# Seven half-width block products in place of eight for each pair of sparse chunks, with half of the second product before it placed between the sixth and the last two

## The reference, cut to what matters

```python
x = _layernorm(x + _L0_attn_ref(x, ...))      # Taylor terms and a gated FFN of width 1248
x = _layernorm(x + _L0_ffn_ref(x, ...))       # the sparse FFN, of width 1792

def _L0_ffn_ref(x, c1_w, c2_w, w1, w2t):
    inter = xf @ c1_w.T @ c2_w.T                                   # rank 16, 1792 scores for each token
    blk = inter.reshape(B * T, n_blocks, SPARSITY)                 # 56 blocks of 32
    idx = jnp.argmax(blk, axis=-1) + jnp.arange(0, INTER, SPARSITY)
    h = jax.nn.relu(jnp.einsum('bkm,bm->bk', w1[idx], xf))
    return jnp.einsum('bk,bkm->bm', h, w2t[idx])
```

## Time and profile before

| what | us |
|---|---|
| median of 3 runs (lowest, highest) | 734.05 (733.7, 734.46) |
| the profiled execution's span | 731.9 |
| TensorE busy in it | 722.7 |
| sparse pairs 0 to 27, from the first block to the last hidden chunk (425.76 to 705.13) | 279.37 |
| from the last hidden chunk to the end of the span | 26.8 |

### The profile page before, as it was taken

The page is one execution under the profiler, slowest core; times in us unless marked ns, Lnnn a source line. Parts: engine busy times, 40 slices in busy tenths (PEclk is TensorE's granted clock), DMA queues, the critical chain, the costliest instruction groups (busy, mean ns, idle before and its releaser), DMA issues.

```text
span 731.9 us, 8884 instructions
## 1 busy us (share of the span) xinstructions
PE 722.7 (99%) x3457; PEld 334.0 (46%) x3457; DVE 480.2 (66%) x930; ACT 214.3 (29%) x341; POOL 157.1 (21%) x131
## 2 busy tenths in 40 slices
PE   8999999999999999999999999999999999999996
PEld 3444444444444444444444444444444444445444
DVE  5978897796877779677767779653755361125136
ACT  1575457435612212122122112122212221122130
POOL 0452443111111111111111111222212212222130
PEclk9999999999999999999999999999999999999999
DMA  9537319310000010100001334104020015001001
GB/s 326 248 124 206 58 15 379 67 48 11 1 17 18 20 20 9 25 20 20 5 19 20 79 81 92 23 4 101 16 75 7 1 29 133 1 0 58 1 1 57
DMA packets 40569, 44.57 MB, mean 61 GB/s; under 512 B 25040, under 2 KB 32848, under 8 KB 39632
## 3 DMA queue, kind: packets, MB, share of 16 engines
q1 hardware_dynamic: 37552, 39.29, 17.9%
q0 software_dynamic: 2112, 4.19, 3.4%
q10 hardware_dynamic: 864, 0.53, 0.2%
HBM read 34.33 MB, written 4.42 MB: 53 GB/s over the span
## 4 chain that ended last, share of the span: by engine, by line
PE 86%; issue 1%; POOL 1%; DVE 0%; ACT 0%
PE acc L469 31%; PE pb L449 24%; PE pa L449 24%; PE acc L775 2%; PE acc L546 2%; PE pick_b L612 1%; PE pick_a L612 1%; POOL big L998 1%; PE pick_a L597 0%; PE pick_b L775 0%; PE acc L465 0%; PE pick_b L465 0%; ACT work L836 0%; ACT work L820 0%; ACT pick_b L821 0%
## 5 line engine op out<-in xcount | busy, mean ns | idle before, releaser
L469 PE MATMUL acc<-big,work 128*128 128x512 f16 x1038 | 234.3, 379 | 0.0
L991 POOL TENSOR_TENSOR work<-work 128x512 f16<-128x512 f32 x92 | 110.2, 1201 | 479.9 <-ACT work L909 270.0
L449 PE MATMUL pa<-xs,big 128*128 128x512 f16 x816 | 188.8, 379 | 0.0
L449 PE MATMUL pb<-xs,big 128*128 128x512 f16 x816 | 187.2, 379 | 0.0
L469 PEld LDWEIGHTS acc<-big,work 128*128 128x128 f16 x1038 | 101.5, 98 | 121.0
L449 PEld LDWEIGHTS pa<-xs,big 128*128 128x128 f16 x816 | 78.6, 98 | 91.8
L449 PEld LDWEIGHTS pb<-xs,big 128*128 128x128 f16 x816 | 78.5, 98 | 91.6
L964 ACT ACTIVATE work<-work 128x512 f16<-128x512 f32 x52 | 32.6, 627 | 203.1 <-DVE work L1611 203.1
L546 PE MATMUL acc<-big 128*128 128x512 f16 x336 | 73.9, 379 | 0.3 <-DVE big L1228 0.2
L1611 DVE SCALAR_TENSOR_TENSOR work<-big,const_sb,pa 128x512 f32<-128x512 f16 x28 | 20.8, 744 | 74.0 <-PE pa L449 67.4
L909 ACT ACTIVATE work<-work 128x512 f16<-128x512 f32 x40 | 25.2, 630 | 143.8 <-DVE work L1365 143.8
(11 more groups left out here) (176 smaller groups left out, 548.8 us busy)
## 6 DMA issues: line engine op xcount, KB each, us to landing
big<-in_w_all SPq DMA_DIRECT2D x2, 3840.0 KB, 17.2
big<-spread_rows SPq DMA_DIRECT2D x16, 448.0 KB, 9.1
big<-in_x_t SPq DMA_DIRECT2D x16, 256.0 KB, 8.7
rows<-in_x POOLq DMA_DIRECT2D x4, 1024.0 KB, 11.8
big<-in_w_all SPq DMA_DIRECT2D x2, 1536.0 KB, 11.2
out<-rows SPq DMA_DIRECT2D x3, 1024.0 KB, 4.3
big<-in_w_all SPq DMA_DIRECT2D x1, 2048.0 KB, 14.4
big<-in_w_all SPq DMA_DIRECT2D x2, 1024.0 KB, 11.6
```

What stands on the lines that cost most here:

```text
L449: mm = nc.tensor.matmul(dst[:, :], weights(wp)(kc * P, P), x_part16(g, xp, kc), start=(kc == 0 and wp == xp), stop=(kc == KC - 1 and wp == 1))
L469: mm = nc.tensor.matmul(acc[t][:, :], act_part(pair, j, ap, t * P, P), weights(wp)(0, H), start=(first and ap == wp), stop=(last and ap == 1))
L991: nc.gpsimd.tensor_tensor(act_part(pair, j, 1), act32[j], act_part(pair, j, 0), ALU.subtract).then_inc(act_lo, 1)
```

## The change

The pair's hidden product, 256 units by 512 tokens over a width of 512, is treated as a 2 by 2 block matrix (two chunks, two halves of the width, two halves of 256 tokens) and made from seven block products instead of eight, after Winograd. A block product (`block_product`) is 2 pieces of the width, three matmuls each, 6 matmuls of 128x128 weights by 256 columns. Four sums of weight blocks for each pair and four sums of x blocks for each group are needed; POOL makes them (`raise_quad`, 6 instructions: two of 512 columns and four of 256), ACT rounds them to float16 (`sums_high`, 1024 columns) and POOL makes the low part (`lower_quad`, 1024 columns): 15 such jobs, of which five are hung in behind phase 1 pairs (11, 12, 17, 18, 19) and ten behind sparse pairs (0 to 5, 8, 9, 15, 16). ACT copies the first block product, then the two of `pb`, then the sum of the next from PSUM (`take_products`), and DVE (two instructions) and POOL (two, `add_products`) combine them into the two chunks in SBUF, on which the mask now works: both of its inputs are in SBUF. The mask's data comes in two halves a group. The scale of these weights is one bit lower.

The core of the diff:

```diff
+SUM_JOBS = (("w", 0), ("w", 1), ("x", 0, 0), ("x", 0, 1), ("w", 2), ("w", 3), ("w", 4), ("w", 5), ("w", 6),
+            ("x", 1, 0), ("x", 1, 1), ("x", 2, 0), ("x", 2, 1), ("x", 3, 0), ("x", 3, 1))
+JOB_IN_SWIGLU = {11: 0, 12: 1, 17: 2, 18: 3, 19: 4}
+JOB_IN_SPARSE = {0: 5, 1: 6, 2: 7, 3: 8, 4: 9, 5: 10, 8: 11, 9: 12, 15: 13, 16: 14}
...
+            def block_product(dst, weights, moving, first=False):
+                for k in range(KH):
+                    for wp, xp in ((0, 0), (0, 1), (1, 0)):
+                        mm = nc.tensor.matmul(dst, weights(k, wp), moving(k, xp), ...)
+                return mm
+
+            def seven_products(g, u, between, after_first, middle):
...
+                if n:
+                    pe.wait_ge(c11_ready, n)
+                block_product(pa[:, low_half], w_block(0, 0), x_block(0, 0), True).then_inc(p1_ready, 1)
+                if n:
+                    pe.wait_ge(c12_ready, n)
...
+                block_product(pb[:, low_half], w_sum(SLOT_S1), x_sum(SLOT_T1), True)
+                block_product(pb[:, high_half], w_sum(SLOT_S3), x_sum(SLOT_T3)).then_inc(p57_ready, 1)
+                if between is not None:
+                    between(KC // 2)
+                pe.wait_ge(p1_taken, n + 1)
+                block_product(pa[:, high_half], w_block(0, 1), x_block(1, 0))
+                block_product(pa[:, low_half], w_sum(SLOT_S2), x_sum(SLOT_T2)).then_inc(p26_ready, 1)
+                if between is not None:
+                    between(KC - 1)
+                if after_first is not None:
+                    after_first()
+                middle()
+                pe.wait_ge(p57_taken, n + 1)
+                block_product(pb[:, low_half], w_sum(SLOT_S4), x_block(1, 1))
+                block_product(pb[:, high_half], w_block(1, 1), x_sum(SLOT_T4)).then_inc(p34_ready, 1)
...
+                seven_products(g, u, between, after_first, lambda: products((0,)))
+                after_hidden()
+                products((1,))
...
+            def take_products(n):
+                act.wait_ge(p1_ready, n + 1)
...
+                act.activation(p1_kept, pa[:, 0:HT], ACT.Copy).then_inc(p1_taken, 1)
...
+                act.activation(p57_kept, pb[:, :], ACT.Copy).then_inc(p57_taken, 1)
...
+                act.activation(q_kept, pa[:, 0:HT], ACT.Copy).then_inc(q_taken, 1)
+
+            def hidden(g, u, high=None, late=False, early=None):
+                take_products(g * U2 + u)
+                if early is not None:
+                    x1_high(early + (GROUPS - 1) * TPG)
                 for j in range(2):
...
                 if high is not None:
                     x1_high(high + (GROUPS - 1) * TPG)
+                if g * U2 + u in JOB_IN_SPARSE:
+                    sums_high(JOB_IN_SPARSE[g * U2 + u])
...
+            def add_products(n):
+                pool.wait_ge(p57_taken, n + 1)
...
+                step(nc.gpsimd.tensor_tensor(p57_sum, p57_kept[:, 0:HT], p57_kept[:, HT:2 * HT], ALU.add))
+                settle()
+                pool.wait_ge(q_taken, n + 1)
+                pool.wait_ge(act_lo, N1 + 2 * n)
+                nc.gpsimd.tensor_tensor(act32[1][:, HT:GT], p57_sum, q_kept, ALU.add).then_inc(c22_ready, 1)
...
+            for n in range(GROUPS * U2):
+                g, u = n // U2, n % U2
+                add_products(n)
+                if n in JOB_IN_SPARSE:
+                    raise_quad(JOB_IN_SPARSE[n])
                 for j in range(2):
...
+                        low(GROUPS * U1 + n, j, m)
+                if n in JOB_IN_SPARSE:
+                    lower_quad(JOB_IN_SPARSE[n])
...
             def mask_hidden(g, u):
+                n = g * U2 + u
+                dve.wait_ge(q_taken, n + 1)
+                dve.wait_ge(act_lo, N1 + 2 * n)
+                v.tensor_tensor(act32[0][:, 0:HT], pa[:, HT:GT], p1_kept, ALU.add).then_inc(c11_ready, 1)
+                dve.wait_ge(p34_ready, n + 1)
+                v.tensor_tensor(work32[:, HT:3 * HT]..., pb[:, :]..., q_kept..., ALU.add).then_inc(c12_ready, 1)
...
                 for j in range(2):
+                    if j:
+                        dve.wait_ge(c22_ready, n + 1)
-                    v.scalar_tensor_tensor(out=act32[j], in0=spread(g, u * 2 + j), scalar=own_rank, in1=(pa, pb)[j][:, :],
+                    v.scalar_tensor_tensor(out=act32[j], in0=spread(g, u * 2 + j), scalar=own_rank, in1=act32[j],
                                            op0=ALU.is_equal, op1=ALU.mult).then_inc(masked, 1)
...
-    nc = bacc.Bacc("TRN2", target_bir_lowering=False, num_devices=1)
+    nc = bacc.Bacc("TRN2", target_bir_lowering=False, num_devices=1, dynamic_dma_scratch_size=4096)
```

More of the change, by code:

```diff
@@ L72 @@
 X1_SCALE = 2.0 ** 9
+TOP2 = 12
 HID_SCALE = 2.0 ** -17
@@ L429, in _ @@
             send(LAST * TPG + 2)
+            sp.wait_ge(masked, C2 + SPREAD_HALVES[0][1])
+            load_spread(2, 0)
             send(LAST * TPG + 3, False)
@@ L683, in _, with second2 @@
             group1(GROUPS - 1)
-            def second2(g, u, kind, after_first):
+            def second2(g, u, kind, after_first, js):
                 before = g * U2 + u - 1
-                for j in range(2):
+                for j in js:
                     c = (u - 1) * 2 + j if kind != "last" else C2 - 2 + j
@@ L697, in second2 @@
                         after_first()
-            def hidden(dst, c, g, between):
-                split_product(dst, lambda part: w2_part(c, 0, part), g, between).then_inc(hid_ready, 1)
-            def unit2(g, u, after_first, after_hidden, after_third, kind, start=False, between=None):
-                for j, dst in enumerate((pa, pb)):
-                    n = g * C2 + u * 2 + j
-                    if not start:
-                        pe.wait_ge(masked, n - 1)
-                    elif j:
-                        pe.wait_ge(swiglu_ready, N1)
-                    hidden(dst, u * 2 + j, g, between if j == 0 else None)
-                    (after_first, after_hidden)[j]()
-                if kind == "phase 1":
-                    before = GROUPS * U1 - 1
-                    for j in range(2):
-                        pe.wait_ge(act_lo, before * 2 + j + 1)
-                        second_product(before, j, lambda part: w1_part(1 - j, 2, part), False, j == 1,
-                                       done=down_ready if j else None)
-                        if j == 0:
-                            after_third()
-                    return
-                if kind != "none":
-                    second2(g, u, kind, after_third)
@@ new lines, in unit2, with last_gated, products @@
+            def unit2(g, u, after_first, after_hidden, after_third, kind, start=False, between=None):
+                def last_gated(j):
+                    before = GROUPS * U1 - 1
+                    pe.wait_ge(act_lo, before * 2 + j + 1)
+                    second_product(before, j, lambda part: w1_part(1 - j, 2, part), False, j == 1,
+                                   done=down_ready if j else None)
+                    if j == 0:
+                        after_third()
+                def products(js):
+                    if kind == "phase 1":
+                        for j in js:
+                            last_gated(j)
+                    elif kind != "none":
+                        second2(g, u, kind, after_third, js)
+                seven_products(g, u, between, after_first, lambda: products((0,)))
+                after_hidden()
+                products((1,))
@@ L778, in second_tile @@
                     mm.then_inc(sparse_ready, 1)
+            unit2(3, 4, none, none, none, "none")
+            for t in range(2):
+                second_tile(3, t, acc[t][:, :])
+            unit2(3, 5, none, none, none, "none")
+            second_tile(3, 2, acc[2][:, :])
+            for h, bank in enumerate(last_halves):
+                second_tile(3, TPG - 1, bank, h * HALF, HALF)
+            unit2(3, 6, none, none, none, "none")
+            for t in range(2):
+                for u in (4, 5):
+                    second_tile(u, t, acc[t][:, :])
+            for t in range(2):
+                second_tile(6, t, acc[t][:, :], done=True)
             for u in (4, 5, 6):
-                unit2(3, u, none, none, none, "none")
-            for t in range(TPG - 1):
-                for u in (3, 4, 5, 6):
-                    second_tile(u, t, acc[t][:, :], done=(u == U2 - 1))
+                second_tile(u, 2, acc[2][:, :], done=(u == U2 - 1))
             for h, bank in enumerate(last_halves):
-                for u in (3, 4, 5, 6):
+                for u in (4, 5, 6):
                     second_tile(u, TPG - 1, bank, h * HALF, HALF, u == U2 - 1)
@@ new lines, in _ @@
+            for u in range(1, GROUPS * U1):
+                low(u, 0, u * 2)
+                if u in JOB_IN_SWIGLU:
+                    raise_quad(JOB_IN_SWIGLU[u])
+                    lower_quad(JOB_IN_SWIGLU[u])
+                low(u, 1, u * 2 + 1)
```

(11 more changed lines are left out.)

188 lines of the change are left out of this document (152 added, 36 removed).

## The result

The changed kernel takes 773.16 us (median of 4 runs), the kernel before 733.88 on the same chip: 1.0515 times as long, with a 95% interval from 1.0485 to 1.0546. The median counts one disturbed run of 1792.7 us; the three others took 768.93, 773.01 and 773.32 us, and the ratio rests on those three alone. I had said 749.0 and a range from 732 to 760. The sign was right and the size was not: 39.3 us lost where 14.9 were forecast.

What follows compares the result with a forecast made beforehand. TensorE was taken as the bound, busy 722.7 of 731.9 us. Terms -16.7 + 9.2 + 5.7 + 7.8 + 3.1 + 5.8 = +14.9 took the median from 734.05 to 749.0 us, range 732 to 760.

Steps and rivals of the forecast that it cites:

- A: z's chain of 3.9 us covered by only 2.59, five tiles, plus z's weight loads: +9.2 us.
- B: Scores 2 wait for the bank that pick 0 frees, 3.7 us against 2.59, five tiles: +5.7 us.
- D: DVE's long runs exceed TensorE's interval: +3.1 us. Also the moment DVE sees the last two block products (`pb`).
- five dense jobs: The five jobs in phase 1 cost nothing, up to 2 us if DVE's picks slip under POOL.
- C: ACT's rounding between the relus and the copy of the first block product, paid in seven pairs: +7.8 us.
- E: POOL's jobs lengthen DVE's two-input SBUF instructions in the long runs: +5.8 us, bounds 0 and 14.
- The gain: Seven products take 4.59 us in place of 5.18, 0.59 less a pair over 28 pairs: -16.7 us.
- the last pairs' second products only change places: 0: At the sparse stage's end, the last second products cover each other, so moving them costs 0.
- The account of one pair behind D: Last relu ends near D + 3.8, P2 (second block product) can start at D + 4.35; the loop has no slack.
- Most small ones fall where POOL waits for its next copy: In DVE's long runs, only a tenth of the small instructions' possible 17.9 us was counted.
- Rival 2: Masks with two SBUF inputs wait for POOL, 10.8 us on top, 760 us; POOL bounds pairs 0 to 5; chance 0.17.
- Rival 1: C, D and E vanish, stalls for z and scores 2 remain: -1.8 us, or -7 (727); chance 0.17 for faster.

Runs made afterwards that it cites:

- run 6: The changed kernel without its fifteen jobs (plain blocks for sums) and with both halves of the second product behind the last two block products: 722.53 us, 0.9853.
- run 5: The changed kernel in its own order without any of the fifteen jobs, plain blocks standing where the sums stood: 742.94 us, 1.0132.
- run 1: The changed kernel without the ten sparse jobs on POOL and ACT, using the sums of phase 1: 747.82 us, 1.0197.
- run 2: The changed kernel without POOL's part of the ten sparse jobs, ACT's rounding kept, sums of phase 1: 750.06 us, 1.0227.
- run 3: The changed kernel with POOL's ten sparse jobs replaced by fills of similar length that read nothing, ACT's rounding kept: 757.7 us, 1.0331.
- run 4: The changed kernel, everything computed, with both halves of the second product behind the last two block products: 752.82 us, 1.0261.

## Why the prediction was wrong in size

Taken apart by the runs, with each step beside the term that I gave it:

| step | predicted | measured | from runs |
|---|---|---|---|
| seven products, both halves behind, no jobs | -16.7 | -10.8 | 6 |
| a half between: A, B and D | +18.0 | +20.4 | 5 and 6 |
| five dense jobs | 0, up to 2 | +4.9 | 1 and 5 |
| ACT's rounding (C) | +7.8 | +2.2 | 1 and 2 |
| POOL beside DVE (E) | +5.8 | +23.1 | 2 and the change |
| sum | +14.9 | +39.8 | |

The sum is 39.8 and not 39.3 because the kernel before measured 733.3 beside run 6 and 733.9 beside the change.

**The gain.** The mechanism held: 9.77 us a pair, six matmuls in 0.66. TensorE's busy time fell by 15.2 us in run 6 (722.7 to 707.5), 1.5 less than the 16.7; 1.3 us went to the waits that run 6 still has; and 2.8 were lost in the tail. The step that failed there is "the last pairs' second products only change places: 0". The last matmul group starts 7.3 us before the end in the kernel before (start 724.60, span 731.9) and 10.1 us before it in run 6 (start 710.66, span 720.8), 2.8 us more. The reason is in the starts of the last normalisations. The first three of the kernel before, from DVE's timeline:

```profile
713.77 0.55 DVE L1445 TENSOR_SCALAR rows<-rows,small 128x512 f32<-128x512 f32 x1
718.95 0.55 DVE L1445 TENSOR_SCALAR rows<-rows,small 128x512 f32<-128x512 f32 x1
724.13 0.55 DVE L1445 TENSOR_SCALAR rows<-rows,small 128x512 f32<-128x512 f32 x1
```

And of the changed kernel (run 6 has the same spacing: 706.33, 710.05, 713.76):

```profile
756.72 0.55 DVE L1662 TENSOR_SCALAR rows<-rows,small 128x512 f32<-128x512 f32 x1
760.43 0.55 DVE L1662 TENSOR_SCALAR rows<-rows,small 128x512 f32<-128x512 f32 x1
764.14 0.55 DVE L1662 TENSOR_SCALAR rows<-rows,small 128x512 f32<-128x512 f32 x1
```

They stood 5.18 us apart before, TensorE's pace, and stand 3.71 apart now, DVE's own. The work that had been the cover was moved ahead.

**A, B and D were right in kind and nearly in size.** z was put at 6.7 us of waits and 2.5 of weight loads, and 7.9 of waits were measured; scores 2 at 5.7 and 3.9 measured; DVE's long runs at 3.1 and the wait for ACT's copy behind them 3.5. Not in the sum were 2.1 us of waits for SP's queue ahead of z and the 3.7 us of longer matmuls. The account of one pair behind D held: the last relu of pair 18 ends 3.80 us after D (670.33 for 666.53), and P2 starts at D + 4.36. Two slips of the working changed little: 3.8 + 0.43 + 0.2 is 4.43 and not 4.35, and five times 1.1 is 5.5 and not 5.7.

**C was too large.** I let ACT's 1.05 us land whole in seven pairs. The wait for ACT did grow by 5.7 us in run 2, but other waits gave 2.0 back and shorter matmuls 2.3, of which 1.7 is the clock's and no merit of the term: waits that stand one behind another in a loop don't add up.

**E is the step that decided.** It had the right mechanism, the right two rows and the wrong share. "Most small ones fall where POOL waits for its next copy" was the failing sentence: with 7.3 us of job in a pair POOL is busy for 11.5 of the 15.46 us behind pair 1 and for 14.1 of the 15.88 behind pair 8, and DVE's chain of small instructions steps through POOL's sums one by one. L1619 and L1621, six each from 442 to 660 us, cost 2.7 and 4.0 us over the 162 ns they have alone (6 x 0.453, 6 x 0.665), the multiply 4.1 (20 x 0.207 over run 1), the `TENSOR_SCALAR`, which I had not counted, 2.1. Of all 23.1 us DVE's own instructions account for most: it is busy for 545.9 us in the change and for 527.4 in run 2, 18.5 more. The term had counted two-input instructions alone; one-input ones are lengthened too, and they carry most of the 7.6 us that fills cost in run 3. Rival 2, "the lock decides", was right in its title and wrong in its place: it laid the wait on the masks, which bear 1.4 us.

**Dense jobs.** "Up to 2" was 4.9. TensorE's waits at the start of the sparse stage show it: 1.8 us for the last multiply of the gated FFN on DVE (L1582 in the changed kernel) there and in run 1, and none in run 5. Another 2.0 us are lost ahead of that: pair 0's first block product starts at 427.60 us in run 1 and at 425.63 in run 5.

**The clock.** "The clock should stay where it is" failed. The change and run 6 issue the same 3961 matmuls and are busy for 717.8 and 707.5 us. So 10.3 of the 50.4 us between their spans are longer matmuls and 40.1 are idle time. In the change the granted clock was 0.50 in four stretches (438.51 to 441.93, 472.65 to 479.47, 564.81 to 568.22 and 650.14 to 653.55 us) with 15.3 us of busy TensorE, in run 6 in none before its last matmul. Half of 15.3 is 7.7 us, which is what the clock cost; the other 2.6 I cannot place, and the modelled ends of matmuls in front of waits may be part of it. This cost is inside the measured terms above: behind a wait like the 2.59 us in front of pair 3 the loss goes on in the matmuls that follow.

**Rival 1** ("only TensorE's own order counts", 732.3) is the change without jobs, and that measured 742.9: the 10.6 between them are the gain's missing 5.9, the 2.4 by which the order costs more than A, B and D, and D itself, which rival 1 left out (3.1), less the 0.7 between the two medians of the kernel before.

With both halves behind, the fifteen jobs cost 30.3 us too (752.82 - 722.53). Against run 6, run 4 loses 5.5 us ahead of pair 0's D (436.52 for 431.02) and 16.3 in the intervals behind pairs 1, 8 and 15 (16.67, 18.33 and 18.63 us for 11.86, 12.59 and 12.89). DVE is busy for 16.1, 17.7 and 18.0 us of these three, so its lengthened instructions set these intervals, and the ones behind them (10.47, 8.32 and 9.54 for 7.60, 7.72 and 6.93) give nothing back.

What stays open: the 25.3 us of the ten sparse jobs were measured whole, and as parts only in the order in which the runs add them; the parts hang together through the clock and need not be the same in another order.

## What to carry to other kernels

Sum the helper work where it runs, not by its engine's share: the ten jobs were 0.8 us in a kernel in which each bank came free a pair later and DVE had slack in a pair, and 25.3 in one in which DVE's, ACT's and POOL's steps stand in the loop. Before TensorE's work is moved ahead of a hand-over, add up the chain that the moved work used to cover (here 3.9 us for z) and leave at least that behind it: the same seven products are 10.8 us faster than before in one order and 9.5 slower in the other, jobs apart. A cheaper product may be worth using only in the pairs where nothing else needs the cover.

## What the runs showed that I had not expected

- Beside fills on POOL, VectorE's instructions with two SBUF inputs keep their 162 ns, and a float32 `TENSOR_SCALAR` with one input goes from 543 to 722, an int32 one of 4 columns from 171 to 1302; beside additions those with two inputs are longer too. Work on POOL that only writes lengthens other instructions than work that reads.
- A kernel whose TensorE waits 53 us in all pays 10.3 us more for the same matmuls than one that is idle for 13, 7.7 of it at half the clock. In the window from 472 to 480 us the granted clock was 0.58 and 0.57 behind four microseconds in which it was busy for 1.41.
- In the kernel before with jobs added, an interval of 13.50 us was followed by one of 7.42: a loop with one pair of slack gives the time back, and only the sum over two pairs tells what a disturbance costs.
